# Attention layer with a gated feed-forward part: value products in runs of two and four, a fourth slot of probabilities, and another order on the vector engine

## The reference

```python
q = concat([split_heads(x @ Wq1), split_heads(x @ Wq2)])      # 32 heads
k2, v2 = repeat(k, 2), repeat(v, 2)                           # of 16 heads
p = softmax(where(causal, q @ k2.T / sqrt(16), min))
y1, y2 = split(p @ v2)                                        # heads 0-15, 16-31
y = (y1 - sigmoid(x @ Wlam) * y2) @ Wo
x = layernorm(x + y)
shared = mlp(x, sh_gate, sh_up, sh_down)                      # 1024 wide, silu(gate) * up
routed = mlp(x, r_gate, r_up, r_down) * comb_w                # 128 wide, comb_w from a top-2 router
x = layernorm(x + shared + routed)
```

## Time and profile before

| what | value |
| --- | --- |
| median of 3 runs | 462.35 us (460.74 to 462.37) |
| the profiled execution's own time | 462.41 us |
| its span, first to last instruction | 460.7 us |
| PE, DVE, ACT, POOL busy | 422.0, 278.3, 237.3, 249.2 us |
| mean granted clock of TensorE | 0.96 |
| iterations 2 to 6, from one group t0 to the next | 51.2 to 51.3 us each |

### The profile page before, as it was taken

The page is one execution under the profiler, slowest core; times in us unless marked ns, Lnnn a source line. Parts: engine busy times, 40 slices in busy tenths (PEclk is TensorE's granted clock), DMA queues, the critical chain, the costliest instruction groups (busy, mean ns, idle before and its releaser), DMA issues.

```text
span 460.7 us, 10485 instructions
## 1 busy us (share of the span) xinstructions
PE 422.0 (92%) x4074; PEld 343.9 (75%) x4074; DVE 278.3 (60%) x679; ACT 237.3 (52%) x536; POOL 249.2 (54%) x335
## 2 busy tenths in 40 slices
PE   4693978899999999999999999999999999997995
PEld 4571447795898669985898679985898579855995
DVE  3256346753758466755857476855767488747464
ACT  4454833467254943577264943486355921493240
POOL 8273636457254944667355935576365921493152
PEclk9796797799999999999999999999999999999998
DMA  7492590354023710372024511380024410000000
GB/s 265 122 267 73 178 257 12 117 140 92 1 69 111 159 47 21 107 179 56 23 81 121 135 47 31 99 208 27 23 85 115 116 47 1 4 1 23 1 25 23
DMA packets 34753, 40.41 MB, mean 88 GB/s; under 512 B 4240, under 2 KB 28304, under 8 KB 34448
## 3 DMA queue, kind: packets, MB, share of 16 engines
q1 hardware_dynamic: 34704, 39.75, 31.8%
HBM read 27.94 MB, written 11.53 MB: 86 GB/s over the span
## 4 chain that ended last, share of the span: by engine, by line
PE 70%; POOL 9%; DVE 8%; ACT 4%; DMA 3%; SPq 3%; issue 2%; POOLq 0%; DVEq 0%; ACTq 0%
PE ff L727 11%; PE ff L728 10%; PE ff L729 10%; PE ring L791 7%; POOL prob L447 6%; PE ybank L873 4%; PE ybank L727 3%; PE ring L786 3%; PE ybank L728 3%; PE ybank L729 3%; PE ring L845 3%; DVE neg_max L1121 2%; PE ff L817 2%; PE ring L727 2%; ACT prob L566 1%
## 5 line engine op out<-in xcount | busy, mean ns | idle before, releaser
L437 POOL TENSOR_TENSOR h_lo<-h_full,h_hi 128x256 fp32r<-128x256 f32 x72 | 53.1, 738 | 100.6 <-ACT h_hi L515 100.6
L1113 DVE TENSOR_REDUCE neg_max<-ring 128x2 f32<-128x384 f32 (+3 forms) x154 | 90.1, 637 | 28.1 <-PE ring L791 27.4
L447 POOL TENSOR_SCALAR_AFFINE_SELECT prob<-prob 128x512 f32<-128x512 f32 x128 | 83.1, 681 | 17.1 <-ACT prob L566 16.2
L727 PE MATMUL ff<-x1T_hi,wg_lo 128*128 128x256 f32 x288 | 87.0, 302 | 0.0
L566 ACT ACTIVATE prob<-ring 128x512 f32<-128x512 f32 x144 | 78.3, 619 | 5.2 <-PE ring L845 5.2
L728 PE MATMUL ff<-x1T_lo,wg_hi 128*128 128x256 f32 x288 | 80.9, 281 | 0.0
L729 PE MATMUL ff<-x1T_hi,wg_hi 128*128 128x256 f32 x288 | 80.8, 281 | 0.0
L1149 DVE COPY yv<-ybank 128x256 f32<-128x256 f32 x64 | 27.0, 422 | 53.1 <-PE ybank L873 52.7
L873 PE MATMUL ybank<-prob,v_ones 128*32 128x256 f32 (+1 forms) x1024 | 56.5, 336 | 2.0 <-POOL prob L447 1.8
L727 PEld LDWEIGHTS ff<-x1T_hi,wg_lo 128*128 128x128 f32 x288 | 54.7, 190 | 3.1 <-issue 1.3
L574 ACT ACTIVATE gate_t<-ff 128x256 f32<-128x256 f32 x72 | 27.7, 385 | 56.0 <-PE ff L729 56.0
(11 more groups left out here) (187 smaller groups left out, 977.1 us busy)
## 6 DMA issues: line engine op xcount, KB each, us to landing
q_stack<-qk_parts_dram SPq DMA_DIRECT2D x48, 256.0 KB, 4.5
qk_parts_dram<-parts SPq DMA_DIRECT2D x72, 128.0 KB
k_stack<-qk_parts_dram SPq DMA_DIRECT2D x48, 128.0 KB, 4.3
xt_raw<-xT SPq DMA_DIRECT2D x8, 256.0 KB, 2.9
xz<-x SPq DMA_DIRECT2D x8, 256.0 KB, 2.9
out<-xz SPq DMA_DIRECT2D x7, 256.0 KB, 2.2
prob<-w_gu SPq DMA_DIRECT2D x1, 1152.0 KB, 6.3
yv<-w_gu SPq DMA_DIRECT2D x1, 1024.0 KB, 7.4
```

The source lines that it names most:

```text
L437: pool.tensor_tensor(h_lo[:, n, :], h_full[:, n % RING, :], h_hi[:, n, :].bitcast(F32), ALU.subtract).then_inc(h_lo_done, 1)
L447: pool.affine_select(out=v, in_=v, compare_op=ALU.is_ge, fill=0.0, base=0, pattern=[[0, 2], [HALF, 2], [0, 2], [1, HALF]], channel_multipl ...
L727: pe.matmul(o, lhs_lo, rhs_hi, start=first, stop=False)
L1113: dve.tensor_reduce(neg_max[:, columns.start:columns.stop, i], ring[u % RING][:, 0:len(columns) * keys].rearrange("p (h k) -> p h k", k=keys),
```

## The change

Four things are altered. First, the order on PE: each t group is issued as before, with gate/up 4 to 6 behind t0 to t2, but the value products now come in runs, pv0 and pv1 behind t3, pv2 and pv3 behind t5, and pv4 to pv7 behind t7 (`PV_BEHIND`). Second, the probabilities get a fourth slot, made of buffers that are idle in this stage: the first two exponentials of groups 3 and 7 go to `rest`, the third to `y1`; group g now waits for the value product of group g-4, and group 3 also for the last use of `rest` and `y1`. Third, DVE does all of units 4, 5 and 6 ahead of the copy of group 0; before, unit 6 came behind that copy and the start of the second norm. Fourth, in the y stage DVE normalizes tile 1 right behind tile 0 and does units 7 and 8 after both; on ACT the high part of the transposed y comes ahead of the rounding of unit 7.

```diff
@@ -57,6 +57,7 @@
 LAST_STEPS = 3
 V_COLS = 32
 RING = 3
+PROB_SLOTS = 4
 STACKS = 2
 X_SLOTS = 3
 REST_SLOTS = 2
@@ -88,6 +89,7 @@
 FF_FIRST, FF_MAX, FF_Y0, FF_Y1 = 0, range(1, 4), 7, 8
 
 FF_SCORES = {0: 4, 1: 5, 2: 6}
+PV_BEHIND = {3: (0, 1), 5: (2, 3), 7: (4, 5, 6, 7)}
 PROJ_CHUNKS = QK_JOBS + 1
 
 SEAM_UNITS = 2
@@ -253,6 +255,15 @@
 
         def first_bank(u):
             return first_banks[u % QUAD]
+
+        def prob_first(g):
+            return rest[:, :, :] if g % PROB_SLOTS == RING else prob[:, g % PROB_SLOTS, 0:2, :]
+
+        def prob_last(g):
+            return y1[:, :, :].rearrange("p t d -> p (t d)") if g % PROB_SLOTS == RING else prob[:, g % PROB_SLOTS, 2, :]
+
+        def prob_unit(g, u):
+            return prob_first(g)[:, u, :] if u < 2 else prob_last(g)
 
         def t_bank(g, u):
             return score_banks[(3 * g + u) % len(score_banks)]
@@ -440,8 +451,8 @@
             def causal(b, groups):
 
                 for g in groups:
-                    first = prob[:, g % RING, 0:2, 0:T].rearrange("p x (i c) -> p x i c", i=2)
-                    last = prob[:, g % RING, 2, :].rearrange("p (x i c) -> p x i c", x=2, i=2)
+                    first = prob_first(g)[:, :, 0:T].rearrange("p x (i c) -> p x i c", i=2)
+                    last = prob_last(g).rearrange("p (x i c) -> p x i c", x=2, i=2)
                     for units, v in ((2, first), (3, last)):
                         pool.wait_ge(exp_done, b * T_UNITS + 3 * g + units)
                         pool.affine_select(out=v, in_=v, compare_op=ALU.is_ge, fill=0.0, base=0,
@@ -561,9 +572,13 @@
             def exps(b, g, units=range(3)):
                 for u in units:
                     act.wait_ge(t_full, b * T_UNITS + 3 * g + u + 1)
-                    if u == 0 and g >= RING:
-                        act.wait_ge(pv_full, b * GROUPS + g - RING + 1)
-                    act.activation(prob[:, g % RING, u, :], t_bank(g, u)[:, :], ACT.Exp, scale=SCALE).then_inc(exp_done, 1)
+                    if u == 0 and g >= PROB_SLOTS:
+                        act.wait_ge(pv_full, b * GROUPS + g - PROB_SLOTS + 1)
+                    if u == 0 and g == RING:
+                        act.wait_ge(qk_l_done, min(b + 2, B) * QK_JOBS)
+                        if not is_first(b):
+                            act.wait_ge(yT_full, b)
+                    act.activation(prob_unit(g, u), t_bank(g, u)[:, :], ACT.Exp, scale=SCALE).then_inc(exp_done, 1)
 
             def gate_tanh(b, n):
                 act.wait_ge(gu_full, b * FF_UNITS + n + 1)
@@ -678,9 +693,9 @@
                 if has_prev:
                     gate_tanh(i - 1, FF_Y0)
                     gate_tanh(i - 1, FF_Y1)
+                yT_first(i)
+                if has_prev:
                     h_first(i - 1, FF_Y0)
-                yT_first(i)
-                if has_prev:
                     h_first(i - 1, FF_Y1)
                 if has_next:
                     values(i + 1, 1)
@@ -867,9 +882,9 @@
                     pe.wait_ge(causal_done, b * (2 * GROUPS) + 2 * g + t + 1)
                     for j in range(4):
                         if t == 0:
-                            p = prob[:, g % RING, j // 2, :].rearrange("p (i h t) -> p h i t", h=2, t=HALF)[:, j % 2, :, :]
+                            p = prob_unit(g, j // 2).rearrange("p (i h t) -> p h i t", h=2, t=HALF)[:, j % 2, :, :]
                         else:
-                            p = prob[:, g % RING, 2, :].rearrange("p (x i h t) -> p x h i t", x=2, h=2, t=HALF)[:, j // 2, j % 2, :, :]
+                            p = prob_last(g).rearrange("p (x i h t) -> p x h i t", x=2, h=2, t=HALF)[:, j // 2, j % 2, :, :]
                         mm = pe.matmul(bank[V_COLS * j:V_COLS * (j + 1), t * P:T], v_ones[:, t, 2 * g + j // 2, :], p,
                                        start=(t == 0), stop=(t == TT - 1))
                 mm.then_inc(pv_full, 1)
@@ -1029,13 +1044,12 @@
                 if not has_prev:
                     pe.wait_ge(stack_loaded, 16 * STACK_LOADS)
                 pe.wait_ge(max_loaded, (i + 1) * (16 * MAX_PARTS))
-                for g in range(GROUPS + 2):
-                    if g < GROUPS:
-                        t_group(i, g)
+                for g in range(GROUPS):
+                    t_group(i, g)
                     if g in FF_SCORES and has_prev:
                         gu_units(i - 1, (FF_SCORES[g],))
-                    if g >= 2:
-                        pv_group(i, g - 2, has_next)
+                    for pv in PV_BEHIND.get(g, ()):
+                        pv_group(i, pv, has_next)
                 if has_next:
                     v_job(i + 1, 0)
                 y_jobs(i, 0)
@@ -1294,12 +1308,11 @@
                         if n == FF_MAX[0]:
                             router_sum(i - 1, *router_steps)
                 if has_prev:
-                    mlp_unit(i - 1, FF_SCORES[0])
+                    for n in FF_SCORES.values():
+                        mlp_unit(i - 1, n)
                 for g in range(GROUPS):
                     if g == 0 and is_first(i):
                         dve.wait_ge(mlp_w_lo_done, W_GATE_UP - 1)
-                    if has_prev and g + 1 in FF_SCORES:
-                        mlp_unit(i - 1, FF_SCORES[g + 1])
                     evacuate_pv(i, g)
                     if has_last:
                         if g == 0:
@@ -1307,10 +1320,9 @@
                         elif g == SCALE_GROUP + 2:
                             second_norm_end(i - 2)
                 normalize_y(i, 0, *attn)
+                normalize_y(i, 1, *attn)
                 if has_prev:
                     mlp_unit(i - 1, FF_Y0)
-                normalize_y(i, 1, *attn)
-                if has_prev:
                     mlp_unit(i - 1, FF_Y1)
                 yT_second(i)
                 if i + 1 < B:
```

More of the change, by code:

```diff
@@ L680, in iteration @@
                     gate_tanh(i - 1, FF_Y1)
-                    h_first(i - 1, FF_Y0)
                 yT_first(i)
                 if has_prev:
+                    h_first(i - 1, FF_Y0)
                     h_first(i - 1, FF_Y1)
```

## The result

**457.5 us**, median of four runs (457.16 to 458.16), against 461.85 for the kernel before in the same session (four runs, 460.74 to 462.37): ratio 0.991 [0.989, 0.993]. The forecast was 458.3 in 456.5 to 462.4, worked out from a time before of 462.35; so 4.1 us of gain were forecast and 4.35 measured. The profiled execution took 457.16 us, span 455.4.

A forecast was written before the change was run, and what follows sets the result against it. PE is busy 92% of the span, but POOL's selects run unbroken into the last value product. Terms 2.6 + 0.03 + 1.4, rounded 4.1 with iteration 7's last copy, from 462.35 give 458.3 us, range 456.5 to 462.4.

The forecast's parts named there:

- Scores ahead of the first value product: Probabilities stage: group 3's scores go first, so its exponentials and selects start 0.52 us earlier; 2.6 us over five iterations.
- The norm in POOL's queue, unit 6 on DVE: Probabilities stage: POOL doesn't wait for the norm statistics, by 0.19; unit 6 ahead removes ACT's 0.29 wait, hidden by idle DVE.
- Do they?: Probabilities stage: whether exponentials keep ahead of POOL; yes, by 0.2 and 0.3 at group 7, with a new ACT wait of 0.46.
- The run of four: pv4 to pv7 on PE: v_job starts at 267.60 instead of 268.12; saved switches yield nothing by themselves.
- The two last copies stay where they were: gain near 0: Iteration 7, without v_job: the last two copies set the transposes and don't move, so gain near 0.
- The y stage: Transposes of tile 0 to input addition: tile 1 ends 0.44 earlier, gain 0.20 in each of seven iterations, 1.4 us.
- (a): Rival: only the y stage pays, exponentials or run of four eat the 0.52; 461.0 us, chance 0.13.
- (b): Rival: only the probabilities stage pays, tile 1 and the low part of y come late; 459.8 us, chance 0.14.
- (d): Rival: slower, ACT starves because t6 is behind pv2 and pv3; about 467 us, or 464 at half, chance 0.08.
- (c): Rival: the second norm on DVE blocks POOL's last select, which ends 0.25 later than before; 462.3 us, chance 0.05.
- (e): Rival: changed PE gaps alter time at 1.2 GHz; 3 us more or fewer shifts the total 1.5, chance 0.08.
- The drain between tiling modes: PE's switches: by rule alone six fewer give 0.4 us per iteration, 2.1 in five; the forecast gave it nothing.

The follow-up runs named there:

- y undone: Kernel after the change with the y stage put back on DVE and ACT: 459.12 us against 461.76 for the kernel before.
- the run of the slot: Kernel after with the old order of value products on PE, keeping fourth slot, unit 6 ahead and new y stage: 460.95 us against 461.96 for the kernel before.
- POOL relieved: Kernel after with unit 6's low part on POOL moved behind all selects: 458.12 us against 461.96 for the kernel before.
- DVE's half: Kernel after with only ACT's old y order, unit 7's rounding ahead of y's high part: 457.98 us against 462.65 for the kernel before.
- three slots: Kernel after with three slots of probabilities instead of four, without the waits for `rest` and `y1`: 477.79 us against 461.76 for the kernel before.
- unit 6 behind: Kernel after with unit 6 on DVE back behind the copy of group 0 and the statistics: 467.02 us against 461.96 for the kernel before.
- alternating kernel: Kernel after without runs of two, pv0 to pv3 each behind its own t group, t3 to t6: 457.91 us against 461.76 for the kernel before.
- both together: Kernel after without runs of two and with unit 6's low part on POOL behind the last select: 455.08 us against 461.96 for the kernel before.

## Why the prediction was right

**Scores ahead of the first value product: right.** 0.52 at the exponentials and selects of group 3 (their starts 7.02 and 8.17 of the stage, forecast 7.03 and 8.19). With y undone the rest is worth 461.76 - 459.12 = 2.6 us, the size forecast, though the interval allows 1.4 to 3.4.

**The norm in POOL's queue, unit 6 on DVE: right**, and the step with most at stake. I had costed the move of unit 6 at nothing, covered by 1.61 of idle DVE, and credited it with 0.29. Undone it costs 1.4 per iteration; with the old order (the run of the slot) it gives nothing. The prediction didn't say that the order hangs on it.

**"Do they?": right in its result.** The forecast slack was 0.2 and 0.3 at the last two selects. In the trace the last two exponentials of group 7 end at 261.53 and 262.02, the selects start at 261.74 and 262.37: 0.2 and 0.35. With POOL relieved this slack was all that could be had, as the two waits there show. ACT's new wait was 0.28 and not 0.46; nothing hung on it.

**The run of four, and that the runs yield nothing: right in iterations 2 to 6** (0.05 without the relief), wrong elsewhere. The sum took the whole change and asked what each iteration gains by it, never what the runs cost where POOL isn't the bound: 0.35 in iteration 1, 0.27 in iteration 7, and 0.45 in iterations 2 to 6 once POOL is relieved.

**"The two last copies stay where they were: gain near 0" failed**, by -0.27 in iteration 7. I took the second norm at its old 1.46. It took 1.15, as the selects beside it now end 0.6 earlier in the stage (the section after next has what ties the two), and the copies followed. The sum held 0.07 for it. The term of 0.52 was short by 0.07 as well, 0.05 of it by POOL's block of selects (5.08 for 5.13).

**The y stage: right**, 0.17 for 0.20. DVE's half needs ACT's: alone it makes B 9.25, 0.10 worse than before. ACT's half alone wasn't run.

**Rivals.** (a) and (b) are refuted by the stretches, (d) didn't occur but was built, with three slots and with unit 6 behind. (c) looked for the block on the wrong engine. Before, the seventh select starts at 266.36 and DVE's instruction at 266.40, and DVE is the one held up, to 267.18; the last select comes in 0.19 ahead of that end and takes 0.05 longer, no more. (e) did occur: the place and number of the stretches at 1.2 GHz go with the difference between 4.3 us by the stages and 5.3 by the spans.

**The number.** That 457.5 was measured and not 458.3 is for 0.5 us the kernel before, 461.85 by four runs where the forecast started from 462.35 by three. That the gain came out so near (4.35 for 4.1) is in part luck: A gave 3.3 where 2.6 was summed, and B gave 1.1 where it was 1.4, in the profiles, one of them with a stretch at 1.2 GHz in it.

**The drain between tiling modes.** By the Trainium skill, "TensorEngine Tiling (Array Packing)", Key Properties, the six saved switches would be PE's gain. The alternating kernel has four of the six again, two pairs at 0.14, and loses 0.05 in iterations 2 to 6, not 0.28; in iterations 1 and 7 it gains 0.35 and 0.27, and with POOL relieved it is the faster one by 0.45. No run here shows more than 0.05 from fewer drains, and none takes them away where PE is the bound of the stage.

## What to carry to other kernels

A queue that never pauses hides another one just behind it: relieving POOL alone gave 0.05 per iteration, ACT alone lost 0.05, both together gave 0.50, so when one relief gives little, look for the wait that took its place and try the pair. Work that is moved ahead "for nothing" may carry the whole change: ask what stands behind it in an in-order queue if it is late. For effects below 0.5%, compare the lengths of the stages in the traces: at 2.4 GHz throughout, A repeated within 0.02 us here and B within 0.08, while the totals of one kernel lay up to six microseconds apart, the longer ones mostly at a lower mean clock.

## What the hardware showed

**DVE beside POOL.** The second norm's two instructions (128x256, SBUF to SBUF) take 0.40 each, 0.73 together, where POOL is idle (above, at 405.57). Together they take 1.15 in the kernel after and 1.46 before. The single instructions of iteration 4 show what makes the difference:

| kernel | POOL's instruction | its end | DVE's start | DVE's end | behind POOL's |
|---|---|---|---|---|---|
| before, first | select | 267.04 | 266.40 | 267.18 | 0.14 |
| before, second | select | 267.71 | 267.11 | 267.86 | 0.15 |
| after, first | select | 263.05 | 262.35 | 263.19 | 0.14 |
| after, second | none | | 263.11 | 263.51 | |
| no runs, second | select | 263.55 | 262.95 | 263.70 | 0.15 |
| POOL relieved, second | low part of h | 265.52 | 264.86 | 265.67 | 0.15 |

DVE's instruction isn't slowed by a factor: it ends 0.14 to 0.16 behind the end of POOL's, however early it started. That holds for all 133 of them, in the 14 profiles, that start while POOL has over 0.1 us of an instruction to go, or at most 0.03 ahead of one. In the kernel with three slots DVE starts first, with no select running. DVE and POOL there, iteration 4:
```profile
275.41 1.08 DVE L1246 TENSOR_SCALAR xz<-xz,ln_mv,ln_t 128x256 f32<-128x256 f32 x2
```
```profile
275.63 1.39 POOL L458 TENSOR_SCALAR_AFFINE_SELECT prob<-prob 128x512 f32<-128x512 f32 x2 [1.15 <-ACT prob L579]
```
The first of the two ends at 275.81 after 0.40, as alone, though a select starts 0.22 into it; the second ends 0.15 behind that select. A select that starts while DVE's instruction runs takes 0.72 instead of 0.68, which is the 0.05 that the eight selects are shorter after the change. So one engine pays nearly all, DVE, and what counts is when POOL's instruction beside it ends. The Trainium skill, "SBUF — State Buffer", Who interferes with whom, has an exclusive lock: who issues first holds the shared ports for the whole instruction, and the other fully blocks. DVE's ends agree with it. For POOL it isn't shown: the select's 0.04 is less than the 0.18 that DVE's instruction had to go.

**The clock.** In a kernel whose PE is busy for over 90% of the span, one wait of 1.56 in a stage of short waits was followed by 3.4 us at 1.2 GHz, in two iterations of five; the other three had the same wait of 1.56 in the same place and kept 2.4 GHz. Such a stretch cost 1.1 us in that stage. That the wait brought it about isn't shown; no other kernel here has one between 100 and 400 us.
